# Other steps for the side jobs of layer 0's experts, and key/value tiles converted in two separate parts

## The reference, cut to what matters

```
h   = layernorm(x) * (1 + cb) + sb
x   = x + gb * ffn0(h)        # ffn0: shared expert + 8 experts, top 2 of a softmax router, exact gelu
                              #   sum_e w[t,e] * (gelu(h @ rw1[e] + rb1[e]) @ rw2[e] + rb2[e]),  hidden 256
h   = layernorm(x) * (1 + ca') + sa'
q, k, v = h @ Wq + bq, h @ Wk + bk, h @ Wv + bv      # layer 1, 16 heads of 8
attn = softmax(k^T v * temperature);  out = q attn   # over 256 tokens of a sequence
```

## Time and profile before

| what | value |
|---|---|
| median of 3 runs | 460.7 us (460.36 to 461.1) |
| profiled execution, its own time | 462.43 us |
| its span, first to last instruction | 460.6 us |
| granted TensorE clock, mean | 0.974 |
| busy: TensorE, VectorE, ScalarE, GpSimd | 411.1, 359.3, 334.5, 253.1 us |
| the expert loop of layer 0 | 65.8 to about 205 us |

### The profile page before, as it was taken

How to read it: one execution, slowest core, us unless ns; L and a number is a source line. 1 busy time by engine, 2 the same in 40 slices (tenths; PEclk the granted TensorE clock), 3 DMA queues, 4 the chain that set the end, 5 groups by cost and what they waited for, 6 DMA issues and landing times.

```text
span 460.6 us, 7995 instructions
## 1 busy us (share of the span) xinstructions
PE 411.1 (89%) x2340; PEld 276.2 (60%) x2340; DVE 359.3 (78%) x891; ACT 334.5 (73%) x898; POOL 253.1 (55%) x276
## 2 busy tenths in 40 slices
PE   8989778899799899889788888979999999999995
PEld 6667566586577667554333333434467787887883
DVE  4768795767898969867988898889966798778763
ACT  4276558798687686677999989999974575675552
POOL 3302238696876677750253446354538875666663
PEclk9899999899999999995999899989999999999999
DMA  6721021131133545561325545421316343432640
GB/s 183 220 74 43 0 76 64 46 95 46 48 113 93 128 122 164 114 109 46 103 47 87 123 116 85 98 74 23 104 27 170 118 138 101 130 114 99 194 123 23
DMA packets 45675, 44.70 MB, mean 97 GB/s; under 512 B 5556, under 2 KB 33788, under 8 KB 45632
## 3 DMA queue, kind: packets, MB, share of 16 engines
q1 hardware_dynamic: 45632, 44.19, 36.1%
HBM read 37.73 MB, written 6.44 MB: 96 GB/s over the span
## 4 chain that ended last, share of the span: by engine, by line
PE 30%; DVE 14%; ACT 7%; DMA 7%; SPq 3%; issue 3%; POOL 1%; POOLq 0%; DVEq 0%; ACTq 0%
PE P L1255 7%; PE P L1257 7%; PE P L1256 7%; DVE nm L911 6%; ACT EX L1192 5%; SPq L342 3%; DMA G<-gate_rows 3%; DMA attention_rows<-O 2%; PE P L1277 2%; PE P L1541 2%; PE P L1529 1%; DMA kv_parts<-kvs 1%; DVE O L926 1%; PE P L1396 1%; DVE kvs L700 1%
## 5 line engine op out<-in xcount | busy, mean ns | idle before, releaser
L470 POOL TENSOR_TENSOR hidl<-tmp,hidh 128x512 fp32r<-128x512 f32 x116 | 149.2, 1294 | 71.8 <-ACT hidh L1144 66.1
L1192 ACT ACTIVATE EX<-P,nm 128x256 f32<-128x256 f32 x256 | 117.2, 509 | 9.0 <-DVE nm L911 8.8
L1144 ACT ACTIVATE hidh<-tmp 128x512 fp32r<-128x512 f32 x116 | 73.1, 630 | 53.4 <-DVE tmp L987 27.9
L911 DVE TENSOR_REDUCE nm<-P 128x4 f32<-128x1024 f32 x64 | 77.9, 1219 | 15.2 <-PE P L1529 14.7
L1255 PE MATMUL P<-XH,WH 128*128 128x512 f32 x176 | 75.8, 431 | 1.3 <-DVE tmp L987 0.9
L1257 PE MATMUL P<-XL,WH 128*128 128x512 f32 x176 | 69.6, 395 | 0.0
L1256 PE MATMUL P<-XH,WL 128*128 128x512 f32 x176 | 69.5, 395 | 0.0
L514 POOL TENSOR_TENSOR qs<-qT,rz 128x128 f32<-128x128 f32 x64 | 25.3, 416 | 73.5 <-DVE rz L919 73.5
L874 DVE TENSOR_TENSOR tmp<-P,G 128x512 f32<-128x512 f32 x64 | 43.4, 686 | 25.9 <-ACT P L1165 15.2
L1192 ACT ACTIVATION_READ_ACCUMULATOR EX<-P,nm 128x1 f32 x256 | 62.2, 243 | 0.0
L1255 PE MATMUL P<-hidh,WH 128*128 128x512 f32 x124 | 50.7, 409 | 11.4 <-POOL hidl L470 9.7
(11 more groups left out here) (140 smaller groups left out, 698.9 us busy)
## 6 DMA issues: line engine op xcount, KB each, us to landing
G<-gate_rows SPq DMA_DIRECT2D x56, 256.0 KB, 3.4
kv_parts<-kvs SPq DMA_DIRECT2D x16, 256.0 KB, 2.9
VS<-kv_parts SPq DMA_DIRECT2D x48, 64.0 KB
KS<-kv_parts SPq DMA_DIRECT2D x48, 64.0 KB
G<-gate_rows SPq DMA_DIRECT2D x8, 224.0 KB, 3.1
G<-gate_rows SPq DMA_DIRECT2D x8, 192.0 KB, 3.2
G<-gate_rows SPq DMA_DIRECT2D x8, 160.0 KB, 2.9
X<-in_x SPq DMA_DIRECT2D x4, 256.0 KB, 3.0
```

The costliest lines, as they stand in the source:

```text
L470: nc.gpsimd.tensor_tensor(hidl[:, u % 3, :], source, hidh[:, u % 3, :].bitcast(fp32), ALU.subtract).then_inc(s["low_ready"], 1)
L911: v.tensor_reduce(nm1[:, g % 4, 2 * h:2 * h + 2, :], P[:, bank:bank + 2, :].rearrange("p j (h s) -> p (j h) s", h=2), AX.X, ALU.max, negat ...
L1144: sc.activation(hidh[:, u % 3, :], source, ACT.Copy).then_inc(s["high_ready"], 1)
L1192: last = sc.activation(ex1(g, j)[:, h * S:(h + 1) * S], P[:, bank_s1(g, j), h * S:(h + 1) * S], ACT.Exp, bias=nm1[:, g % 4, j, h:h + 1], a ...
```

## The change

The change gives several side jobs of the loop other steps. On VectorE `router_weights` part 0 goes from i = 7 to 6, `ln_apply(1)` from 15 and 16 to 13 and 15, `add_experts` from 5 to 7, `ln_stats(2)` from 6 and 8 to 7 and 8, `ln_apply(2)` from 10 and 11 to 11 and 12. Of the second and third tile that follow in quarters 2 and 3, `kv_values` now stands at i = 3 and 5, and `kv_parts` at 4 and 6, where `kv` did both at 4 and 6. On ScalarE `router_exp` goes from 6 to 5 and `queries_out` from 16 to 17. On TensorE `weights_back` goes from 13 to 12, `tokens_back` from 5 to 6, `transpose_tokens(2)` from 15 to 14, and the second `project_kv` of a quarter from 3 to 2. Nothing is added or taken away.

```diff
--- before.py
+++ after.py
@@ -876,23 +876,23 @@
                 if p + 1 < NP:
                     if i == 4:
                         router_logits(0, p + 1)
-                    if i in (7, 9, 10):
-                        router_weights(0, p + 1, (7, 9, 10).index(i))
+                    if i in (6, 9, 10):
+                        router_weights(0, p + 1, (6, 9, 10).index(i))
                 if p + 2 < NP:
                     if i in (1, 4):
                         ln_stats(1, p + 2, i // 4)
-                    if i in (15, 16):
-                        ln_apply(1, p + 2, i - 15)
+                    if i in (13, 15):
+                        ln_apply(1, p + 2, i // 2 - 6)
                 if p >= 1:
 
                     if i == 3:
                         gate_experts(0, p - 1)
-                    if i == 5:
+                    if i == 7:
                         add_experts(0, p - 1)
-                    if i in (6, 8):
-                        ln_stats(2, p - 1, i // 2 - 3)
-                    if i in (10, 11):
-                        ln_apply(2, p - 1, i - 10)
+                    if i in (7, 8):
+                        ln_stats(2, p - 1, i - 7)
+                    if i in (11, 12):
+                        ln_apply(2, p - 1, i - 11)
                     if i == 17 and p == 1:
 
                         dve.wait_ge(s["ld_w1"], 16 * N_LD["ld_w1"])
@@ -901,8 +901,12 @@
                         link(last)
                     if i == 17:
                         kv(TPP * (p - 1))
-                if p >= 2 and i in (0, 4, 6):
-                    kv(TPP * (p - 2) + (1, 2, 3)[i // 3])
+                if p >= 2 and i in (3, 5):
+                    kv_values(TPP * (p - 2) + i // 2 + 1)
+                if p >= 2 and i in (4, 6):
+                    kv_parts(TPP * (p - 2) + i // 2)
+                if p >= 2 and i == 0:
+                    kv(TPP * (p - 2) + 1)
 
             def maxima(g, h):
 
@@ -1171,14 +1175,14 @@
                         modulate(1, p + 1)
                     if i == 3:
                         high_input(0, p + 1)
-                    if i == 6:
+                    if i == 5:
                         router_exp(0, p + 1)
                     if i == 13:
                         weights_out(0, p + 1)
                 if p >= 1:
                     if i == 15:
                         modulate(2, p - 1)
-                    if i == 16:
+                    if i == 17:
                         queries_out(p - 1)
             high0(NP * STEPS0 - 1)
 
@@ -1505,18 +1509,18 @@
                         transpose_tokens(1, p + 1, MISC)
                     if i == 4:
                         route(0, p + 1)
-                    if i == 13:
+                    if i == 12:
                         weights_back(0, p + 1)
                 if p >= 1:
-                    if i == 5:
+                    if i == 6:
                         tokens_back(0, p - 1)
-                    if i == 15:
+                    if i == 14:
                         transpose_tokens(2, p - 1, MISC)
                     if i == 16:
                         project_q(p - 1)
                     if i == 17:
                         project_kv(2 * p - 2)
-                if p >= 2 and i == 3:
+                if p >= 2 and i == 2:
                     project_kv(2 * p - 3)
 
             def scores(g, half):
```

## The result

| | before | after |
|---|---|---|
| median of 5 runs | 460.7 us (458.28 to 463.24) | 468.5 us (465.35 to 469.36) |
| profiled execution, its own time | 462.43 us | 465.35 us |
| its span | 460.6 us | 463.5 us |

The changed kernel takes 1.0176 of the time of before, 95% interval [1.0128, 1.0223]: some 8 us more. 462.4 us had been forecast, in a range of 458.6 to 464.6. The direction was right, the size was not, and the time is outside the range.

What follows compares the result with a forecast made beforehand. TensorE was taken to bound the kernel, its 3 to 4 us of idle time a quarter set by VectorE's job list. -0.7 - 0.4 + 3.6 - 0.8 = +1.7 us on 460.7 gave 462.4 us, range 458.6 to 464.6.

Steps and rivals of the forecast that it cites:

- The bound and the chain: Whole loop: TensorE is fullest, with 3 to 4 us idle a quarter; its waits come from VectorE's list of jobs.
- W asked for one step earlier: TensorE behind W: transposition 0.35 plus up and down group 1.40; p = 0 -0.7, p = 1 -0.4, p = 2 +3.6 us.
- The end of p = 3: Last quarter, to step 16: earlier transfer of G against a later step 3 multiplication, -0.8 us (bounds -2.4 to +1.2).
- the wait for G: Step 16 of p = 3: the multiplication stood 3.59 us for G's transfer; TensorE's new 1.2 us wait lies beside it.
- The terms of p = 2: Third quarter: W 2.7 us later, step 14 4.1 later, less 0.5 for later waits: +3.6 us (bounds 0 to +5).
- wait, exponential, list and W in a row: p = 2: project_kv wait 2.2 us for 0.6, table loads at 146.0, VectorE's list 2.7 later, W at 161.3.
- absorbed: Rival: project_kv waits are taken out of later waits and VectorE catches up; no change, 460.7 us; chance 0.22.
- Faster: Rival: two-part tile fills idle time and avoids GpSimd, project_kv wait under 1 us in p = 2; 458.8 us; chance 0.28.
- An exponential that gains in p = 0 and 1: router_exp a step earlier: in p = 0 and 1 everything up to W comes about 1.4 us sooner.
- The shared lock: VectorE blocked by GpSimd: a tile's second part was put at 0.8 to 1.9 us in p = 2's list.

Runs made afterwards that it cites:

- experiment 4: The changed kernel with 8 filler products on TensorE while it waits for W in p = 1 and 2: 464.39 us, ratio to before 1.0107.
- experiment 5: The changed kernel with project_kv back at step 3 and the tiles whole at steps 4 and 6: 461.44 us, ratio to before 1.0071.
- experiment 2: The kernel before with only the second project_kv of p = 2 and 3 at step 2 instead of 3: 465.02 us, ratio 1.0129.
- experiment 8: The kernel before with only kv_values at steps 3 and 5, kv_parts at 4 and 6, project_kv at 2: 464.61 us, ratio 1.0141.
- experiment 3: The changed kernel with weights_back at step 13 again: 466.86 us, ratio to before 1.0128.
- experiment 7: The kernel before with only router_exp at step 5 and router_weights part 0 at step 6: 459.55 us, ratio 1.0019.
- experiment 9: The kernel before with router_exp at step 5 and router_weights part 0 at 6 in p = 0 and 1 only: 458.28 us, ratio 0.9955.
- experiment 1: The kernel before with only weights_back at step 12 instead of 13: 462.37 us, ratio 1.0079.
- experiment 12: The kernel before with the change's moves except project_kv, tiles, weights_back, and with transpose_tokens(2) kept at step 15: 460.05 us, ratio 1.0027.
- experiment 11: The kernel before with router_exp and router_weights part 0 early in p = 0 and 1, and key-bias products at step 14 of p = 1: 458.20 us, ratio 0.9972.
- experiment 6: The changed kernel with project_kv, the tiles and weights_back where they stood before: 461.76 us, ratio to before 1.0063.
- experiment 10: The kernel before with the two key-bias products at step 14 of p = 1 instead of 17: 460.29 us, ratio 1.0011.

## Why the prediction was wrong in size

Loop times of p = 0, 1, 2 and 3 changed by -0.2, +0.7, +5.3 and +1.4; the forecast had -0.7, -0.4, +3.6 and -0.8.

**The bound and the chain were read rightly.** The new waits came where they were put and with their size: 1.96 us at `project_kv` in p = 2 (2.2 forecast), 1.02 in p = 3 (1.2), 2.6 to 2.7 for W in p = 1 and 2. W was ready 29.6 us after the first group of p = 2, where it had been 26.3: 3.2 later (2.7 forecast, with 3.3 as the upper bound), and 1.3 earlier in p = 1 (1.4 forecast). In p = 0 it was 0.8 earlier instead of 1.4, with the low clock of 72 us ahead of it; in experiments 4 and 5, without that, it was 1.4.

**The failed step is "W asked for one step earlier".** It counted behind W a transposition and 1.40 us for the up and down group. That is a duration at 2.4 GHz. The clock appeared in that step as a gain for p = 0 alone, and the possibility that a wait of 2 to 3 us would take it away was not in the sum, although had the 0.94 of p = 0, where TensorE had just waited 1.9 us. The traces without the low clocks tell what the step would have given: p = 0 at 30.2 (-0.8, forecast -0.7), p = 1 at 34.7 (-0.7, forecast -0.4), both in experiments 4 and 5, and p = 2 at 39.8 (+3.9, forecast +3.6), in experiment 4. So the low clocks are 3.3 us of the loop: 0.5, 1.4 and 1.4. The fall is not certain: behind the waits of 2.5 to 2.7 us for W it came in three of three traces in p = 2 without filler and in one of three in p = 1. A wait of under 2 us was followed by it in some traces and not in others (1.96 at `project_kv`: in experiments 2 and 8, not in the changed kernel, 3 and 4). How many low clocks the other four runs of the changed kernel had, no trace shows; their mean granted clocks, 0.966 to 0.974, lie around the 0.972 of the traced one.

**"The end of p = 3" had the wrong sign as well,** -0.8 where +1.4 was measured. Two of its statements fell. The first: the wait of 1.2 us was said to lie beside the wait for G. It does not; it shifts VectorE's whole list (experiment 2: +1.3 for a wait of 1.02), and the last down product of the loop ended 39.0 us after the quarter's first group, where it was 37.4 before. The second: an earlier transfer of G was to shorten the quarter. Experiments 7 and 9 and the kernel before have the same code in p = 3; the multiplication of step 16 came 32.3 us after the first group before, and 30.1 and 30.0 there, without a wait for G, and the last down product ended at 37.4 in all three. So the 3.59 us of the earlier trace rows belonged to one execution and were not in TensorE's path. The tiles' second parts meeting GpSimd (4.9 us for the two) don't explain the loss either: in experiment 5 they took 4.9 us too, and p = 3 was 27.9.

With these two put right, 2.2 for p = 3 and 3.3 for the clock, the forecast of 462.4 would have been 467.9, against 468.5.

**The terms of p = 2 were not told apart.** I had them as wait, exponential, list and W in a row. Alone on the kernel before, `project_kv` at step 2 makes +3.9 (experiment 2), the exponential +1.4 (7), W's step +1.6 (1). These can't be added: experiment 1 contains a low clock behind W and experiment 2 one behind `project_kv`, and the changed kernel has the first alone. Within the changed kernel the tile's part is worth 1.3 us (experiment 5 against it), the low clock 1.4 (experiment 4), and what is left is 2.6: the exponential and the later sum and norm, which by themselves make 2.7 (experiment 12). These are the 5.3; asking for W a step earlier costs p = 2 nothing besides the clock.

**Of the rivals,** "absorbed" was true of the wait for W in p = 1 of experiment 1, and is out for `project_kv` by experiment 2, in which nothing was given back in p = 3. "Faster" named its own test, a wait under 1 us at `project_kv`, and failed it; the two parts bring next to nothing (8). An exponential that gains in p = 0 and 1, as it had, is what experiments 9 and 11 keep.

**The shared lock** cost more than I took: the second parts of the two tiles in p = 3 took 2.4 and 2.5 us, 0.7 each where undisturbed, against the 0.8 to 1.9 for one that went into the list of p = 2 (where it took 1.8). That VectorE's copies in a two-port mode and its instructions with two SBUF inputs can be held up by GpSimd is the rule of the Trainium skill ("SBUF — State Buffer", section "Who interferes with whom"). The trace agrees: L701, with two inputs, takes 0.42 or 1.4 to 1.5 us, and the copy L700 0.3 to 1.33.

**What stays open.** The runs after are 7.8 us over before and the loop's table explains 7.0. Loop and medians agree within 1 us in experiments 1, 2, 4, 5, 6, 8, 9 and 12; they do not in 3 (+4.2 and +7.2), 7 (-1.4 and 0.0), 10 (-0.8 and +0.3) and 11 (-3.8 and -1.8). Each loop time is that of one execution, and runs of one kernel spread over 7 to 11 us there. Why the clock falls behind one wait and not behind an equal one is not shown.

## What to carry to other kernels

When a request of the full engine is moved ahead, count from when its answer is ready: everything queued behind it waits too, and the engine that it feeds loses its work in turn. Such a wait may be given back later (W in p = 1 of experiment 1) or not (`project_kv` in p = 3), and it can bring a low clock behind it, here for 1.4 us; put that into the sum with a chance of its own. A job that hides in another engine's table loads is cheap only as long as it stands ahead of them in the order; here, moving the loads ahead gained in the quarters with little such work and lost in the one with much. And before two traces are compared, look where each has its low clocks: a difference in a part that nobody edited is not the edit's.

## What the runs showed of the hardware

Code ahead of the loop that is the same in all kernels ended between 63.8 us (after) and 67.2 us (experiment 9). In the attention, the stretch from VectorE's copy of the 19th group's result to that of the 25th (25.7 us before) took 23.8 to 23.9 in seven traces and up to 30.2 in that of experiment 4. The row of the waits that stands out there, of experiment 4:

```profile
POOL SC L524 <- DMA SC<-attention_rows: 5.5, 1, 5.5
```

GpSimd waits for the attention rows to come back through DRAM, between nothing and 5.5 us over the traces: at most 1.7 us in the seven, 2.5 in before, 4.7 in experiment 11 and 5.5 here, so the stretch grows with it. The clock is low in the window around it (0.67 from 300 to 310 us):

```profile
290.00:300.00 10.00, 10.00 (x90) 4.42 (x87) 7.74 (x18) 10.00 (x46) 1.56 (x4) 1.00 0.46 79
300.00:310.00 10.00, 4.97 (x36) 1.63 (x28) 5.61 (x14) 6.30 (x27) 5.13 (x8) 0.67 0.43 122
310.00:320.00 10.00, 9.02 (x69) 3.61 (x66) 8.87 (x31) 8.01 (x31) 3.08 (x6) 0.81 0.00 0
```

Before's own runs spread from 454.8 to 466.4 us. A comparison of two single profiles of this kernel by their spans is therefore worth little, while stretches of the loop repeat to 0.1 us where nothing was changed and the clock doesn't fall (p = 3: 27.8 in six traces; p = 0 with the early exponential: 29.4 in experiments 7 and 11, but 30.3 in 9, where the clock fell).
